# Conv and mixture-of-experts block on one core: the second matmul's W2 read in place at a register's address

## What is computed

```python
probs = softmax(xf @ gate_w + gate_b)
top2_vals, top2_idx = top_k(probs, 2)
def step(acc, params):                      # for each of 8 experts
    w1, bb1, w2, bb2, we = params           # w1 128x256, w2 256x128
    h = gelu(xf @ w1 + bb1, approximate=False)
    y = h @ w2 + bb2
    return (acc + we[:, None] * y, None)
x = x + out
```

## Time and profile before

| | us |
|---|---|
| median of three executions | 403.15 |
| lowest and highest | 402.12, 404.54 |
| span of the profiled execution (first to last instruction) | 400.1 |
| TensorE matmuls busy in it | 315.2 |
| GpSimd busy | 228.9 |
| VectorE busy | 227.3 |
| ScalarE busy | 195.6 |

### The profile page before, as it was taken

How to read it: one execution, slowest core, us unless ns; L and a number is a source line. 1 busy time by engine, 2 the same in 40 slices (tenths; PEclk the granted TensorE clock), 3 DMA queues, 4 the chain that set the end, 5 groups by cost and what they waited for, 6 DMA issues and landing times.

```text
span 400.1 us, 9901 instructions
## 1 busy us (share of the span) xinstructions
PE 315.2 (79%) x2395; PEld 264.9 (66%) x2395; DVE 227.3 (57%) x988; ACT 195.6 (49%) x526; POOL 228.9 (57%) x351
## 2 busy tenths in 40 slices
PE   0999799999999999999999995049989797885000
PEld 0354688888889888898898994038867686774000
DVE  3983257878778787787887876502222122332085
ACT  1253566565565665756656652314444444442063
POOL 4013043777777777777777766204777777777300
PEclk9999899999999999999999999558999999999555
DMA  8958612222222222222222220855777777762298
GB/s 209 274 164 249 265 54 75 89 80 100 78 93 85 82 99 78 90 94 76 98 84 83 95 80 26 145 139 169 223 222 243 230 231 232 227 221 72 82 315 234
DMA packets 52450, 57.88 MB, mean 145 GB/s; under 512 B 6892, under 2 KB 40423, under 8 KB 52424
## 3 DMA queue, kind: packets, MB, share of 16 engines
q1 hardware_dynamic: 45031, 48.16, 39.1%
q0 software_dynamic: 4544, 8.44, 6.6%
q10 hardware_dynamic: 2848, 0.99, 1.4%
HBM read 30.70 MB, written 14.97 MB: 114 GB/s over the span
## 4 chain that ended last, share of the span: by engine, by line
PE 53%; SPq 16%; issue 10%; DMA 6%; ACT 4%; DVE 4%; POOL 2%; ACTq 2%; DVEq 1%; POOLq 0%
PE bank L1326 18%; PE bank L1315 15%; SPq L481 5%; PE bank L1248 5%; SPq L490 4%; SPq L496 3%; DMA wide<-result 2%; PE bank L1279 2%; PE bank L1433 2%; ACT samp L758 2%; PE bank L1269 2%; PE bank L1260 2%; POOL result L658 2%; DMA routed<-padding_sb 1%; DMA result<-y,to 1%
## 5 line engine op out<-in xcount | busy, mean ns | idle before, releaser
L658 POOL DMA_INDIRECT result<-y,to x78 | 76.8, 985 | 43.8 <-DVE to L1191 26.8
L1326 PE MATMUL bank<-filt_sb,samp 128*128 128x128 f32 x576 | 79.3, 283 | 4.1 <-ACT samp L758 2.5
L1326 PEld LDWEIGHTS bank<-filt_sb,samp 128*128 128x128 f32 x576 | 69.1, 191 | 18.1 <-ACT samp L758 14.2
L1315 PE MATMUL bank<-S,xwin 100*128 100x144 f32 x512 | 78.9, 298 | 1.8 <-issue 1.7
L602 POOL DMA_INDIRECT routed<-payload,slot x64 | 63.2, 987 | 18.5 <-issue 13.5
L758 ACT ACTIVATE samp<-bank 128x432 f32<-128x432 f32 (+1 forms) x96 | 46.3, 484 | 52.8 <-PE bank L1315 52.8
L1315 PEld LDWEIGHTS bank<-S,xwin 100*128 100x128 f32 x512 | 67.7, 193 | 2.2 <-issue 2.0
L923 DVE TENSOR_TENSOR S<-ysp,bank 100x512 f32<-100x512 f32 (+1 forms) x96 | 52.5, 550 | 22.9 <-ACT ysp L729 21.8
L1433 PE MATMUL bank<-rowsT,w_blk 128*128 128x256 f32 x156 | 44.4, 408 | 13.3 <-DMA w_blk<-w_all 10.2
L1199 DVE TENSOR_TENSOR y<-bank,w_blk 128x256 f32<-128x256 f32 x39 | 16.6, 425 | 66.0 <-PE bank L1442 64.2
L822 ACT ACTIVATE rowsT<-bank 128x256 f32<-128x256 f32 x39 | 15.0, 384 | 61.0 <-PE bank L1424 61.0
(11 more groups left out here) (110 smaller groups left out, 493.1 us busy)
## 6 DMA issues: line engine op xcount, KB each, us to landing
w_blk<-w_all SPq DMA_DIRECT2D x39, 321.0 KB
xwin<-lines SPq DMA_DIRECT2D x64, 120.0 KB
xwin<-lines SPq DMA_DIRECT2D x32, 160.0 KB
rows_in<-routed SPq DMA_DIRECT2D x39, 129.0 KB
wide<-result SPq DMA_DIRECT2D x16, 256.0 KB, 4.8
w_all<-in_experts SPq DMA_DIRECT2D x4, 642.0 KB, 7.4
out_tiles<-res SPq DMA_DIRECT2D x8, 256.0 KB, 4.6
wide<-in_x_rows SPq DMA_DIRECT2D x3, 512.0 KB, 8.6
```

The costliest lines, as they stand in the source:

```text
L658: nc.gpsimd.indirect_dma_start(result, bass.IndirectOffsetOnAxis(to[:, slot, j:j + 1].bitcast(U32), 0), y[:, slot, j, :], None, bounds_che ...
L1315: last = nc.tensor.matmul(bank[5 + (par + g) % 2][:, i * TAPS * TT:(i + 1) * TAPS * TT], xwin[:, par, t, :], weights[:, t], start=True, st ...
L1326: last = nc.tensor.matmul(bank[7][:, 0:C], samp[:, par, j, :], filt_sb[:, order[j], :], start=(j == 0), stop=(j == TAPS - 1))
```

## The change

The weights of an expert are laid out as W1, b1, b2, W2, and the copy to `w_blk` takes the first three alone (`W_KEPT` floats of `WROW`, 386 of 642). The moving side of `down` is then `w_all[:, expert, ...]`, where `expert` stands in a register of TensorE. For that TensorE loads block rows from `blk_i` into registers itself: three after the first up of turn 0, four after the first up of every looped turn (for the last block of the turn before and the first three of this one), three in the short last turn, and one ahead of the last down. It waits once for the plan, ahead of the first transposes. VectorE takes b2 at its new place in the slot.

```diff
-W_UP = HID + HALVES
-WROW = W_UP + HALVES * C + C
+W_B2 = HID + HALVES
+W_KEPT = W_B2 + C
+WROW = W_KEPT + HALVES * C
...
-        w_blk = sb("w_blk", [P, RING, WROW])
+        w_blk = sb("w_blk", [P, RING, W_KEPT])
...
-                sp.dma_start(w_blk[:, slot, :], w_all[:, expert, :]).then_inc(w_arrived[slot], 16)
+                sp.dma_start(w_blk[:, slot, :], w_all[:, expert, 0:W_KEPT]).then_inc(w_arrived[slot], 16)
...
-                b2_row = w_blk[:, slot, WROW - C:].unsqueeze(1).broadcast_to([P, SUBS, C])
+                b2_row = w_blk[:, slot, W_B2:].unsqueeze(1).broadcast_to([P, SUBS, C])
...
-            def down(turn, place):
+            def experts_of(first, n):
+
+                _, rows = nc.values_load_multi_w_load_instructions(
+                    blk_i[0:1, bass.ds(first, n)], engines=[mybir.EngineType.PE],
+                    min_val=0, max_val=IDLE_ROW)
+                return [nc.s_assert_within(row >> REGION_BITS, 0, EXPERTS - 1) for row in rows]
+
+            def down(turn, place, expert):
...
-                                                w_blk[:, slot, W_UP + h * C:W_UP + (h + 1) * C],
+                                                w_all[:, expert, W_KEPT + h * C:W_KEPT + (h + 1) * C],
...
-            def block_step(turn, place):
-                up(turn, place)
-                if not is_last(turn, place):
-                    transpose_rows(turn, place + 1)
-                if not is_first(turn, place):
-                    down(*previous(turn, place))
-
+            def blocks(turn, n):
+
+                begun = is_first(turn, 0)
+                for place in range(n):
+                    up(turn, place)
+                    if place == 0:
+                        experts = [None] + experts_of(0, n - 1) if begun else experts_of(turn * RING - 1, n)
+                    if not is_last(turn, place):
+                        transpose_rows(turn, place + 1)
+                    if place > 0 or not begun:
+                        down(*previous(turn, place), experts[place])
+
+            pe.wait_ge(s.plan_ready, 1)
             transpose_rows(0, 0)
-            block_loop(pe, block_step)
-            down(TURNS, REST - 1)
+            blocks(0, RING)
+            with pe.Fori(1, TURNS) as turn:
+                blocks(turn, RING)
+            blocks(TURNS, REST)
+            expert, = experts_of(BLOCKS - 1, 1)
+            down(TURNS, REST - 1, expert)
```

More of the change, by code:

```diff
@@ L1473 @@
         np.asarray(L0_ffn_b1).reshape(EXPERTS, HALVES, P).transpose(2, 0, 1),
+        np.broadcast_to(np.asarray(L0_ffn_b2), (P, EXPERTS, C)),
         w2.reshape(P, EXPERTS, HALVES * C),
-        np.broadcast_to(np.asarray(L0_ffn_b2), (P, EXPERTS, C)),
     ], axis=2)
```

## The result

The changed kernel takes 418.55 us (median of four executions, 417.40 to 419.79) against 403.38 us (402.12 to 404.54) for the kernel before: ratio 1.038, 95% interval [1.035, 1.042]. It is slower by 15.2 us, and the time lies above the range of the forecast, 402.2 to 411.5 us, which had its likeliest case at 404.4 us. The profiled execution takes 419.79 us, the longest of the four, and spans 417.9 us; the one before spans 400.1 us.

A forecast was written before the change was run, and what follows sets the result against it. GpSimd's back-to-back sends bound the kernel, 10.32 us a turn against TensorE's forecast 10.2; +0.7 at the start and +0.5 in the first turn, +1.2 us on the 400.1 us span, plus 3.05 to the median, gave 404.4 us, range 402.2 to 411.5.

The forecast's parts named there:

- the price of a batch of four: TensorE's four register loads with range checks and shifts, priced from SyncE's short loads: 3.1 us, 2.3 us more per turn.
- The cover: Matmuls queued while a batch's registers load: 0.87 us of up plus 0.1 of rest, hiding 0.97 of 3.1 us.
- the first rival: TensorE's register work becomes the pace: idle over 2.4 us per turn, excess paid in eight turns; 406.3 to 414.4 us; 0.33.
- 0.55 against 0.33: Chances given to the sends staying the pace (0.55) and to TensorE's register work becoming the pace (0.33).
- the first turn: The first batch of four costs 2.3 against y of block 3 being 1.8 early: GpSimd late by 0.5 us, once.
- the 1.8 of reserve: How early block 3's y is for its send on GpSimd: 1.8 us, called the small reserve of the chain before the sends.
- they do not pace the end: Weight copies pace TensorE (10.2 us of waits) but not the kernel's end; SyncE waits only 0.2 us for a slot.
- a rival of its own at 421 us: TensorE's clock falls to half for one block per turn after a batch's idle time: 17 us, about 421 us; chance 0.05.
- The sends bind: GpSimd's 78 sends stand back to back, 10.32 us per turn of four blocks; nothing earlier than its send shortens this.
- the dear end "the load waits for the array": First rival's dearest case: TensorE's load gets no cover from queued matmuls, 3.3 us per turn, +11.2 us, 414.4 us; 0.06.
- the first term: The start: the batch of three delays block 0's chain and so the first send, +0.7 us, ends 0 and +2.5.
- TensorE's waits for copies mostly gone: Sign of being right: TensorE's copy waits mostly vanish, replaced by about 2 us idle per turn before the transposes.

The follow-up runs named there:

- run 3: The kernel before (whole copies, W2 read from its slot) with the change's batches of register loads added, their values unused: 424.77 us, ratio 1.052.
- run 5: The change with registers loaded two at a time, behind the ups of places 0 and 2 of a turn: 406.51 us, ratio 1.005.
- run 7: The change with weight copies released without waiting for y, and b2 read from expert 0 for every block: 415.48 us, ratio 1.031.
- run 2: The change with the up ahead of each batch done four times (twice in turn 0), keeping the array busy: 415.22 us, ratio 1.026.
- run 4: The change without its registers: short copy, W2 read in place at expert 0's fixed address for all blocks: 403.84 us, ratio 0.999.
- run 1: The change with each expert's register loaded on its own, ahead of the up of its block: 404.67 us, ratio 1.002.
- run 8: The change with batches of four without shifts, copies released without waiting for y, and b2 from expert 0: 405.00 us, ratio 1.003.

## Why the prediction was wrong

**The step that failed is the price of a batch of four**, "0.1 for the address, 0.87, 4 x 0.28, 4 x 0.23". Of the terms, the register operations were nearly right and the load was not: 1.31 us for 0.87. The prediction had SyncE's loads of up to 1357 ns before it, took the short ones because the chain shows a long one behind an issued copy and "TensorE issues none", and kept the long ones for a rival. (For the operations: from 290.9 to 294.54 us is 3.64, less 0.1 and 1.31 is 2.2 us, where 2.14 was priced.) The cover held: the first address operation starts at 290.9, the priced 0.1 ahead of the up at 290.99. So the load's 0.44 and the operations' 0.1 made a turn longer by 2.85 us and not by 2.3.

The load's 0.44 can be taken apart in part. The batch of three at the start of the stage and the batch at 291 us, each load with the DMA traffic during it (stretch, length, PE busy, PEclk, DMA share, GB/s):

```profile
L1440 PEldq TENSOR_LOAD <-blk_i x1: 789/789/789, 266.5 to 266.5; - x1
```

```profile
266.47:267.26 0.79, 0.79 (x2) 0.50 0.00 0
291.00:292.31 1.31, 1.02 (x6) 1.00 0.81 242
```

With no traffic at all three registers took 0.79 us where 0.67 was priced. With one at 0.31 that is 0.24 for each further one, so an estimate for four is 1.03; the quickest load of four in the stage took 1.01, at 328.2 us. So some 0.16 us lie in the price taken from SyncE, and the other 0.28 came in mid-stage, where the loads of four take up to 1.36. What adds them isn't isolated; that the loads of run 3, beside more traffic, are longer is a sign of the traffic, and not a proof.

The decision point of the first rival was 2.4 us more per turn, so a difference of half a microsecond moved the kernel from one case to the other. A forecast that stands 0.1 us inside a limit, with a term borrowed from another engine, was a coin toss, and 0.55 against 0.33 was too sure.

**The rival had the mechanism, but its price stopped short.** "Each excess is paid in eight turns" gives 8 x 0.45 = 3.6, 1.0 for the first turn (2.85 less the 1.8 of reserve) and 0.7 at the start: 5.3 us, 408.5, still inside the range. Run 5, with an excess of 0.2 per turn, fits that working (1.8, 0.8 for the first turn, and the start; measured 2.3, with an interval from 1.0 to 3.0). The change does not, because two more things followed here:

- The copies. The prediction read SyncE's wait of 0.2 us as "they do not pace the end". It was a state, and not a property: a copy is released by the y of the block four before it, and SyncE issues in order. Once y lost its reserve this wait grew to 25.0 us, and with SyncE's own register loads and the landing behind it TensorE lost 4.1 us. Run 7, which frees the copies, has 2.8 us less of these waits and is 3.1 us faster, in part by shorter loads and one fall of the clock less.
- The clock. It had a rival of its own at 421 us with a chance of 0.05, which the range left out; the four falls cost 7.3 to 7.8 of the 15.5 us. What spoke against it, a stretch with 1.04 us of matmuls in 3.2 at 1.00, has its like in the change (316 to 319 us, 1.08 us, 1.00), while other batches were followed by 0.50. The rule of the Trainium skill's page "TensorE: Matmul & The Clock Gate", "HAM oscillation", that idle stretches between groups of matmuls can throttle the array again each time, is what four of the turns show, at 1.2 GHz; the others don't. Run 2, with the array kept busy through the batches, has one fall, and its rest is 1.4 us; run 5, whose gaps are at most 1.1 us, has none between 280 and 370 us.

**What held.** The sends bind and nothing that comes sooner shortens the kernel: run 4 has the copies' gain alone, and it is 0. Reading W2 at a register's address cost nothing that shows: run 1 has all of it, ratio 1.002 with an interval up to 1.004. A load does run beside the matmuls: in the batch above it starts at 291.0 us, with the first matmul of the up, and the 3.64 us of register work end where the transposes start. Nor is the load long because it waits for the array: in run 2, with 3.72 us of matmuls queued, it takes no longer.

```profile
L1440 PEldq TENSOR_LOAD <-blk_i x11: 310/1298/1392, 268.5 to 381.4; - x11
```

What the Trainium skill's page "Perfetto Trace Analysis", "Sequencer Loop", has of control instructions agrees with these traces, and the dear end "the load waits for the array" can be crossed out. The start cost 1.6 us, of which 0.73 lie ahead of the stage, as the first up shows, 266.47 against 265.74. The remaining 0.9 is near the 0.7 of the first term. "TensorE's waits for copies mostly gone" came true in the change (4.1 for 10.2), but not for the reason given: in run 4, which has the short copies alone, they stayed at 8.3.

**What stays open.** Why the clock fell after some batches and not after others of the same length is not settled, and so neither is how much of the loss would stay with the clock at 1.00 throughout. That the batches are the cause is shown by runs 1 and 3, and that a gap costs little once TensorE's pace is at or under the sends' by runs 5 and 8. How the 15.2 us divide into pace, late copies and clock is read from the traces: run 7 takes out most of the waits for copies and run 2 most of the falls, but each moves another share with it.

## What to carry to other kernels

TensorE, which here reads registers from a table in its own queue, is idle for as long as its sequencer works beyond the matmuls already queued, 2.5 us per batch: load one register per block under a block's matmuls, and not four at once, even if that means more loads. Where a forecast rests on one pace being a tenth of a microsecond under another, give both cases the same chance, and follow the slower case further than its first order: which ring, which queue and which clock were hidden by the reserve that is then gone. A wait of 0.2 us in a profile tells that a resource is ready in time now, not by how much.

## What the runs showed of the hardware

- A load of registers on TensorE takes longer with their number: in the medians of the runs 0.31 us for one, 0.78 for two (run 5, below), 1.31 for four, 1.59 for four beside the whole copies. Without DMA traffic three took 0.79. SyncE's short 0.27 and 0.47 for one and two were too low a price for a batch on TensorE.

```profile
L1440 PEldq TENSOR_LOAD <-blk_i x21: 313/777/914, 267.9 to 369.4; - x21
```

- Matmuls whose moving side has its address in a register cost the array nothing here: the block from 308.63 to 310.61 us in run 5 is the packed 1.98 us.
- The clock can fall to 1.2 GHz in the middle of a stage where it was 1.00 before (from 280 to 362 us), and gaps of the same length did not always bring it down: 0.50 from 296 to 299 us, 1.00 from 316 to 319, behind idle times of 2.52 and 2.61 us.
